# The last attention step and the first feed-forward blocks in an order of their own, and feed-forward products in groups of four

## The reference

```python
def attn(x):      # linear attention, 32 heads of 8
    q, k, v = split(relu(x @ qkv_weight.T))
    vk = einsum('bnhe,bnhd->bhed', concat(v, 1), k)
    o = einsum('bhed,bnhd->bnhe', vk, q)
    return (o[..., :8] / (o[..., 8:] + 1e-15)) @ proj_weight.T + proj_bias

def xattn(x, ctx):    # softmax attention over the context, 16 heads of 16, rotary positions
    q, k, v = rope(x @ Wq.T), rope(ctx @ Wk.T), ctx @ Wv.T
    return softmax(q @ k.T * 0.25) @ v @ Wo.T + bo

def ffn(x):       # both layers of low rank: 256 -> 64 -> 1024 -> 64 -> 256
    P = x @ U1
    H = gelu(P @ V1 + b1)          # tanh form
    return (H @ U2) @ V2 + b2

x = layernorm(x + attn(x))
x = layernorm(x + xattn(x, ctx))
x = layernorm(x + ffn(x))
```

## Time and profile before

| | |
|---|---|
| time, median of 3 runs | 579.31 us (578.76 to 579.71) |
| profiled execution, its time | 579.79 us |
| its span in the trace | 578.0 us |
| TensorE busy | 517.7 us, 90% |
| VectorE, GpSimd, ScalarE busy | 390.9, 341.1, 319.4 us |
| mean granted TensorE clock | 0.963 |

### The profile page before, as it was taken

How to read it: one execution, slowest core, us unless ns; L and a number is a source line. 1 busy time by engine, 2 the same in 40 slices (tenths; PEclk the granted TensorE clock), 3 DMA queues, 4 the chain that set the end, 5 groups by cost and what they waited for, 6 DMA issues and landing times.

```text
span 578.0 us, 11456 instructions
## 1 busy us (share of the span) xinstructions
PE 517.7 (90%) x4044; PEld 350.5 (61%) x4044; DVE 390.9 (68%) x870; ACT 319.4 (55%) x457; POOL 341.1 (59%) x391
## 2 busy tenths in 40 slices
PE   6995998999999999999999999999777786899992
PEld 3884666666767676767667676767453343555551
DVE  6468786878787878778787878787776331334444
ACT  3452556565666656575656566565564562455641
POOL 6567266595959595766858595948553312242424
PEclk9999899999999999999999999999797798899998
DMA  8653111203021211112030202111010010122322
GB/s 270 140 109 82 43 34 57 69 7 100 10 78 32 77 51 36 59 49 88 5 102 10 78 30 78 33 38 33 1 33 20 2 54 18 55 99 100 110 92 108
DMA packets 29128, 35.96 MB, mean 62 GB/s; under 512 B 5720, under 2 KB 15320, under 8 KB 29080
## 3 DMA queue, kind: packets, MB, share of 16 engines
q1 hardware_dynamic: 28216, 34.37, 19.8%
q10 hardware_dynamic: 864, 0.95, 0.7%
HBM read 23.51 MB, written 8.65 MB: 56 GB/s over the span
## 4 chain that ended last, share of the span: by engine, by line
PE 60%; DVE 15%; issue 13%; POOL 5%; ACT 5%; DMA 1%; POOLq 1%; SPq 0%; DVEq 0%; ACTq 0%
PE FR L1187 21%; PE BK L1353 10%; PE BK L1187 8%; DVE nmax L1006 5%; PE SC L1310 5%; PE SC L1338 4%; PE FR L1270 3%; PE FR L1262 3%; PE FR L1381 3%; DVE lin_tm L916 2%; POOL rs L630 2%; POOL c_fm L635 2%; PE SC L1187 2%; DVE x_fm_l L993 2%; DVE rden L912 1%
## 5 line engine op out<-in xcount | busy, mean ns | idle before, releaser
L738 ACT ACTIVATE probs<-SC 128x1024 f32<-128x1024 f32 x128 | 131.1, 1024 | 103.1 <-PE SC L1338 103.0
L1006 DVE TENSOR_REDUCE nmax<-SC 128x4 f32<-128x1024 f32 x128 | 155.9, 1219 | 24.9 <-PE SC L1310 23.8
L1353 PE MATMUL BK<-probs,v_aug 128*32 128x256 f32 x1024 | 71.1, 396 | 0.6 <-ACT probs L738 0.6
L543 POOL TENSOR_TENSOR rs<-ve,minus_half 128x2 f32<-128x2 f32 x16 | 11.2, 701 | 94.3 <-DVE nm L1054 94.3
L1310 PE MATMUL SC<-k_blk,q_grp 48*128 48x512 f16 x256 | 51.2, 397 | 15.6 <-DVE nmax L1006 15.6
L1338 PE MATMUL SC<-q_grp,k_blk 64*128 64x256 f16 x512 | 51.1, 278 | 4.3 <-ACT probs L738 2.2
L827 ACT ACTIVATE probs<-SC,b_ff 128x512 f32<-128x512 f32 x64 | 39.9, 685 | 24.1 <-PE SC L1535 23.2
L1353 PEld LDWEIGHTS BK<-probs,v_aug 128*32 128x32 f32 x1024 | 27.1, 111 | 26.8 <-issue 15.5
L630 POOL TENSOR_TENSOR rs<-ve,minus_half 128x2 f32<-128x2 f32 x16 | 11.0, 689 | 47.8 <-DVE nm L1175 47.8
L1338 PEld LDWEIGHTS SC<-q_grp,k_blk 64*128 64x128 f16 x512 | 25.1, 97 | 22.7 <-ACT probs L738 6.2
L1545 PE MATMUL FR<-probs,w_u 128*64 128x512 f32 x128 | 36.7, 628 | 0.7 <-ACT probs L827 0.7
(11 more groups left out here) (229 smaller groups left out, 1546.1 us busy)
## 6 DMA issues: line engine op xcount, KB each, us to landing
x_fm<-in_x_fm SPq DMA_DIRECT2D x16, 256.0 KB, 5.4
x_tm<-in_x_tm SPq DMA_DIRECT2D x16, 256.0 KB, 5.1
x_kept<-x2b SPq DMA_DIRECT2D x16, 256.0 KB, 2.3
x_tm<-x_kept SPq DMA_DIRECT2D x16, 256.0 KB, 2.7
out<-c_fm SPq DMA_DIRECT2D x16, 256.0 KB, 2.0
c_fm<-in_c_fm SPq DMA_DIRECT2D x15, 256.0 KB, 5.8
k_blk<-k_rope SPq DMA_DIRECT2D x128, 16.0 KB, 1.8
cos_t<-rope_tables SPq DMA_DIRECT2D x8, 128.0 KB
```

The lines of the kernel that those rows point to most:

```text
L738: act.activation(probs[:, j % 4], SB[:], ACT.Exp, scale=SCALE).then_inc(s_exp, 1)
L1006: dve.tensor_reduce(nmax[:, t, :, 2 * q:2 * q + 2], src[:].rearrange("p (s f) t -> p s f t", s=2), AX.X, ALU.max, negate=True).then_inc(s_ ...
L1353: mm = pe.matmul(BK[q // 2][HP * k:HP * (k + 1), (q % 2) * T:(q % 2 + 1) * T], v_aug[b % NB][:, t, HC * q + k], probs[:, j % 4, k], start= ...
```

## The change

- The last step of the first stage (sequence 15) is taken out of the loop of steps and written out for each engine (`last_step`). In it the scores of chunk j go to `SC[j % 2]`, SA and SB in turn, and wait for exp j-2 instead of exp j-1. The parts of sequences 13 and 14 get other places; `wo(14)` writes FR[0] instead of BK[1].
- Feed-forward blocks 0 and 1 are both written out, mixed with the end of sequences 14 and 15; the loop starts at block 2. The two products of `h_ff(0, 0)` and `(0, 1)` stand before `pv(15, 6)` and `pv(15, 7)`. The gelu table is loaded by an instruction of its own behind the last exp.
- In a block, TensorE's order becomes h 0 to 3 of block i, u2 4 to 7 of block i-1, h 4 to 7 of i, v2 of i-1, u2 0 to 3 of i. Each u2 product has its own `wait_apart`. `ev_qf(i-1)` moves behind gelu 3 of block i.
- `gel` takes all of `probs`: eight buffers.
- VectorE's `ev_p(15)` moves behind block 0; the counts of s_y3, s_qf_ev and s_u2_mm start at zero.

The diff (without the 8 spaces that all its lines begin with):

```diff
@@ -182,7 +182,7 @@
-gel = probs[:].rearrange("p s h t -> p s (h t)")[:, :, 0:FB]
+gel = early.rearrange("p (g t) -> p g t", t=FB)
 qf_fm = [t[:].rearrange("p c t -> p (c t)") for t in xs_fm]
 x2_blk = x_tm
 y3 = x_fm
@@ -427,7 +427,7 @@
     def ffn_block(i, more=True):
         for h in range(2):
             if more:
-                sp.wait_ge(s_y3, 2 * i + h + 3)
+                sp.wait_ge(s_y3, 2 * i + h + 1)
                 fetch(i + 1, h)
         for h in range(2):
             sp.wait_ge(s_y, 4 * i + 2 * h + 2)
@@ -614,12 +614,16 @@
     weights_lo(V1, s_ff_lo)
     weights_lo(DD2, s_ff_lo)
     residual_bias(2)
-    for b in range(B):
+    for b in range(LAST):
         step(b)
+    norm2(LAST - 2)
+    att_scale(LAST - 1)
+    att_lo(LAST - 1)
+    keep_x2(LAST - 2)
     att_scale(LAST)
     norm2(LAST - 1)
+    att_lo(LAST)
     keep_x2(LAST - 1)
-    att_lo(LAST)
     norm2(LAST)
     keep_x2(LAST)
@@ -735,7 +739,7 @@
             act.wait_ge(s_ff_lo, 2)
         act.wait_ge(s_s2_mm, NQ * b + j + 1)
         wait(act, s_pv_mm, NQ * b + j - 3)
-        act.activation(probs[:, j % 4], SB[:], ACT.Exp, scale=SCALE).then_inc(s_exp, 1)
+        act.activation(probs[:, j % 4], (SC[j % 2] if b == LAST else SB)[:], ACT.Exp, scale=SCALE).then_inc(s_exp, 1)
     def step(b):
         n, m, p, q = b + 2, b + 3, b - 1, b - 2
@@ -817,38 +821,62 @@
     ev_x1(1, FR[1])
     ev_q2(1)
     ev_lint(2, FR[1])
-    for b in range(B):
+    def last_step():
+        exp_chunk(LAST - 1, 7)
+        ev_shift(LAST)
+        exp_chunk(LAST, 0)
+        exp_chunk(LAST, 1)
+        ev_x2t(LAST - 2)
+        exp_chunk(LAST, 2)
+        exp_chunk(LAST, 3)
+        ev_p(LAST - 2)
+        exp_chunk(LAST, 4)
+        ev_att(LAST - 1)
+        exp_chunk(LAST, 5)
+        exp_chunk(LAST, 6)
+        exp_chunk(LAST, 7)
+    for b in range(LAST):
         step(b)
-    exp_chunk(LAST, 7)
+    last_step()
+    act.preload_act_table(ACT.Gelu_apprx_tanh)
     act.sem_inc(s_gelu, 4)
     def gelu(i, f):
-        wait(act, s_u2_mm, NF * i + f + 1)
+        if not isinstance(i, int) or i > 0:
+            act.wait_ge(s_u2_mm, NF * i - NF + f + 1)
         act.wait_ge(s_h_mm, NF * i + f + 1)
-        act.activation(gel[:, f % 4], SC[f % 4 // 2][:].rearrange("p h t -> p (h t)")[
+        act.activation(gel[:, f], SC[f % 4 // 2][:].rearrange("p h t -> p (h t)")[
             :, FB * (f % 2):FB * (f % 2) + FB], ACT.Gelu_apprx_tanh,
             bias=b_ff1[:, f:f + 1]).then_inc(s_gelu, 1)
     def ev_qf(i):
-        act.wait_ge(s_u2_mm, NF * i + NF + 4)
+        act.wait_ge(s_u2_mm, NF * i + NF)
         act.activation(qf_fm[0][:], FR[0][:], ACT.Copy).then_inc(s_qf_hi, 1)
+    act.wait_ge(s_pv_mm, NQ * B - 2)
+    for f in range(4):
+        gelu(0, f)
     act.wait_ge(s_pv_mm, NQ * B)
-    gelu(0, 0)
-    gelu(0, 1)
+    gelu(0, 4)
     ev_att(LAST)
-    for f in range(2, 6):
+    for f in range(5, NF):
         gelu(0, f)
     ev_x2t(LAST - 1)
-    gelu(0, 6)
     ev_p(LAST - 1)
-    gelu(0, 7)
+    for f in range(4):
+        gelu(1, f)
+    ev_qf(0)
+    for f in range(4, NF):
+        gelu(1, f)
     ev_x2t(LAST)
     ev_p(LAST)
-    with act.Fori(1, NFB) as i:
+    with act.Fori(2, NFB) as i:
+        for f in range(4):
+            gelu(i, f)
         ev_qf(i - 1)
-        for f in range(NF):
+        for f in range(4, NF):
             gelu(i, f)
     ev_qf(NFB - 1)
@@ -1041,11 +1069,11 @@
         wait(dve, s_attt_ev, p)
         dve.transpose(flat(att_raw[:]), flat(lin_tm[:])).then_inc(s_att_raw, 1)
-    def add2(p):
+    def add2(p, src=BK[1]):
         dve.wait_ge(s_wo_mm, p + 1)
         dve.wait_ge(s_x1b, p + 1)
         wait(dve, s_x2, 2 * p)
-        dve.tensor_tensor(y2[:], BK[1][:].rearrange("p (t c) -> p t c", t=TT), x1b[:, p % NB], ALU.add
+        dve.tensor_tensor(y2[:], src[:].rearrange("p (t c) -> p t c", t=TT), x1b[:, p % NB], ALU.add
                           ).then_inc(s_wo_ev, 1)
     def stats2(p):
@@ -1145,18 +1173,23 @@
     row_max(0, 6)
     row_max(0, 7, SB)
     shift(0)
-    for b in range(B):
+    for b in range(LAST):
         step(b)
-    dve.sem_inc(s_qf_ev, 1)
-    dve.sem_inc(s_y3, 2)
+    ev_shift(LAST)
+    stats2(LAST - 2)
+    turn_pv(LAST - 1, 1)
+    att_norm(LAST - 1)
+    att_turn(LAST - 1)
+    ev_p(LAST - 2)
+    turn_pv(LAST, 0)
+    add2(LAST - 1, FR[0])
     turn_pv(LAST, 1)
     att_norm(LAST)
+    stats2(LAST - 1)
     att_turn(LAST)
-    stats2(LAST - 1)
+    ev_p(LAST - 1)
     add2(LAST)
-    ev_p(LAST - 1)
     stats2(LAST)
-    ev_p(LAST)
     def ffn_block(i):
         dve.wait_ge(s_qf_hi, i + 1)
@@ -1170,10 +1203,11 @@
             dve.tensor_tensor(y3[:, h], BK[h][:].rearrange("p (t c) -> p t c", t=TT), x2_blk[:, h], ALU.add
                               ).then_inc(s_y3, 1)
         for h in range(2):
-            stats(y3[:, h], (s_y3, 2 * i + h + 3), st3[:, h], s_st3, mv3[:, h], s_mv3, 4 * i + 2 * h)
+            stats(y3[:, h], (s_y3, 2 * i + h + 1), st3[:, h], s_st3, mv3[:, h], s_mv3, 4 * i + 2 * h)
             dve.tensor_scalar(ve3[:, h], mv3[:, h, :, 1], LN_EPS, None, ALU.add).then_inc(s_ve3, 1)
             dve.tensor_scalar(nm3[:, h], mv3[:, h, :, 0], -1.0, None, ALU.mult).then_inc(s_ve3, 1)
     ffn_block(0)
+    ev_p(LAST)
     with dve.Fori(1, NFB) as i:
         ffn_block(i)
@@ -1329,13 +1363,17 @@
     def scores2(b, j):
         q, t = j // 2, j % 2
+        out = SC[j % 2] if b == LAST else SB
         if j == 0:
             pe.wait_ge(s_shift_ev, 2 * b + 2)
-        wait(pe, s_exp, NQ * b + j)
+        if b < LAST:
+            wait(pe, s_exp, NQ * b + j)
+        elif j > 0:
+            pe.wait_ge(s_exp, NQ * b + j - 1)
         for f in range(2):
             for s in range(2):
                 rows = slice(TR * s, TR * (s + 1))
-                mm = pe.matmul(SB[:, 2 * s + f], k_blk[b % NB][rows, q, f, t * P:(t + 1) * P],
+                mm = pe.matmul(out[:, 2 * s + f], k_blk[b % NB][rows, q, f, t * P:(t + 1) * P],
                                q_grp[b % NB][rows, q], start=True, stop=True)
         mm.then_inc(s_s2_mm, 1)
@@ -1347,20 +1385,24 @@
             pe.wait_ge(s_v2_ev, min(b + 2, B))
             if on(b + 3):
                 pe.wait_ge(s_q1_ev, b + 4)
-        if j == 4:
+            if b == LAST:
+                pe.wait_ge(s_pvc_ev, b)
+        if j == 4 and b < LAST:
             wait(pe, s_wo_ev, b)
+        elif j == 4:
+            pe.wait_ge(s_pvd_ev, b)
         for k in range(HC):
             mm = pe.matmul(BK[q // 2][HP * k:HP * (k + 1), (q % 2) * T:(q % 2 + 1) * T],
                            v_aug[b % NB][:, t, HC * q + k], probs[:, j % 4, k],
                            start=(t == 0), stop=(t == TT - 1))
         mm.then_inc(s_pv_mm, 1)
-    def wo(p):
+    def wo(p, out=BK[1]):
         if p == 0:
             pe.wait_ge(s_qo_lo, 2)
         pe.wait_ge(s_attt_ev, p + 1)
         for t in range(TT):
-            mm = project(BK[1], att_fm, w_o2, t)
+            mm = project(out, att_fm, w_o2, t)
         mm.then_inc(s_wo_mm, 1)
     def x2_t(q):
@@ -1518,13 +1560,33 @@
     scores1(0, 6)
     scores1(0, 7)
     proj1(2)
-    for b in range(B):
+    def last_step():
+        scores2(LAST - 1, 7)
+        shift_t(LAST)
+        scores2(LAST, 0)
+        scores2(LAST, 1)
+        pv(LAST - 1, 6)
+        pv(LAST - 1, 7)
+        scores2(LAST, 2)
+        x2_t(LAST - 2)
+        scores2(LAST, 3)
+        pv(LAST, 0)
+        pv(LAST, 1)
+        p_ff(LAST - 2)
+        scores2(LAST, 4)
+        scores2(LAST, 5)
+        pv(LAST, 2)
+        pv(LAST, 3)
+        scores2(LAST, 6)
+        scores2(LAST, 7)
+        pv(LAST, 4)
+        pv(LAST, 5)
+        wo(LAST - 1, FR[0])
+    for b in range(LAST):
         step(b)
-    scores2(LAST, 7)
-    pv(LAST, 6)
-    pv(LAST, 7)
-    pe.sem_inc(s_u2_mm, 4)
+    last_step()
     pe.wait_ge(s_ff_lo, 2)
     def h_ff(i, f):
@@ -1536,20 +1598,29 @@
                            start=(k == 0), stop=(k == 1))
         mm.then_inc(s_h_mm, 1)
-    def u2_ff(i, f):
-        for k in range(2):
-            pe.wait_ge(s_gelu, NF * i + f + k + 5)
-            if f + k == 0:
-                pe.wait_ge(s_qf_ev, i + 1)
-            pe.matmul(FR[0][R * k:R * k + R, :], w_u2[:, f + k], gel[:, (f + k) % 4],
-                      start=(f == 0), stop=(f == NF - 2)).then_inc(s_u2_mm, 1)
+    def h_ff4(i, half):
+        for f in range(4 * half, 4 * half + 4):
+            h_ff(i, f)
+    def u2_ff4(i, half):
+        if half == 0 and isinstance(i, int) and i == 0:
+            pe.wait_ge(s_wo_ev, LAST)
+        elif half == 0:
+            pe.wait_ge(s_qf_ev, i)
+        for f in range(4 * half, 4 * half + 4):
+            wait_apart(pe, s_gelu, NF * i + f + 5)
+            pe.matmul(FR[0][R * (f % 2):R * (f % 2) + R, :], w_u2[:, f], gel[:, f],
+                      start=(f < 2), stop=(f >= NF - 2)).then_inc(s_u2_mm, 1)
     def v2_ff(i):
-        pe.wait_ge(s_qf_ev, i + 2)
+        pe.wait_ge(s_qf_ev, i + 1)
```

(44 more changed lines are left out.)

## The result

The median is **556.34 us** (four executions, 555.81 to 557.4) against 579.43 before (four): ratio 0.9605, 95% interval 0.9587 to 0.9623. The forecast was 564.8, in a range from 561.3 to 569.0. The direction was right, and the change gave 23.1 us where 14.5 were forecast. The profiled execution took 557.4 us, the slowest of its four, 1.06 above the median.

The account below looks back on a forecast made before the run. Order bound the stretch from 452 to 501, TensorE's own work the loop. The last block's u2 end moved from 566.0 to 550.0, 16.0 us raw; less 0.7 and 0.8, gain 14.5: forecast 564.8 us, range 561.3 to 569.0.

Parts of the forecast that it names:

- the signs of being wrong: ScalarE idle over 2 us between exps 3 and 4, u2 group over 2.5 us, or v2, `wo(15)`, `x2_t(15)` waiting.
- The last step: Sequence 15's eight exps: alternating score buffers and written order end them at 466.0 against 470.72, 4.7 us earlier.
- Last exp to the first qf copy: Stretch behind the last step: table load right behind the last exp, one TensorE wait; 17.3 us against 26.22 before.
- the hole of 1.7: TensorE's single wait, before the transpose of sequence 14, for POOL's norm ready at 474.1: 1.7 us.
- the 1.5 us given back: Taken off the raw gain of 16.0 us: 0.7 for uncounted handovers, 0.8 for half clock behind TensorE's wait.
- The loop: Feed-forward blocks on TensorE: 9.64 us against 9.88, fewer changes between h and u2, each u2 group about 2.03.
- The bound: Cross-check from 452.3 to 566.0: TensorE's work at full clock is 91.3 us, so no order gains over 22.4.
- A: Whole kernel, the forecast itself: the new order holds, 562.5 to 567 us; chance 60%.
- B: Behind the last exp: load 1.46 us late, TensorE at half clock twice more, 568.8 us; chance 20%.
- C: Feed-forward blocks get no shorter, or slip because qf's low half comes late: 566.5 us; chance 8%.
- D: Last step: exps stay 2.3 us apart as ScalarE waits for `x2_t` and `p_ff`; 4.7 us lost, 569.5; chance 7%.
- E: u2 products: the semaphore instruction stops pairs overlapping, 0.6 x 32 pairs = 19 us, 584 us; chance 5%.

Follow-up runs that it names:

- filler: Changed kernel with five unused products of 512 columns on TensorE behind `shift_t(15)`, in the lull before the last step: 556.83 us median.
- v2 later: Kernel before, with v2 of the block before placed behind h 6-7 instead of h 4-5 in the loop: 580.81 us median, ratio 1.0043.
- the statistics early: Changed kernel with `stats2(14)`, `norm2(14)` and `ev_x2t(14)` moved ahead of `turn_pv(15, 1)`, `att_scale(15)` and gelus 5 to 7: 554.45 us median.
- the best kernel: Changed kernel with statistics of 14 ahead of the turn of 15, no table load of its own, `ev_x2t(13)` behind exp 2: 554.23 us median, ratio 0.9595.
- the one-buffer run: Changed kernel with the last step's scores all in SB, waiting for exp j-1 again, written order kept: 560.37 us median, ratio 0.9679.

## Why the prediction was wrong

**The reading of what bounds** was right. The order ahead of the loop carried the most (7.0 + 9.0 of 22.4 us), and the loop is bound by TensorE. The range reached down to 561.3 by allowing for no handovers, no clock fall and a last step 2 us shorter, and all three came true. What took the time below it is the loop, for which the range had nothing, and 2.0 us of clock and of the profiled executions' places (1.4 and 0.6). None of the signs of being wrong showed: ScalarE idled 0.45 us between exps 3 and 4, a u2 group took 1.87, and neither v2 nor `wo(15)` nor `x2_t(15)` waited. All of them looked for a slower kernel, none for a faster one.

**The last step**: mechanism right, the term mis-sized. I took half clock up to 460.6 "as before". In the profile it was 3.4 us, in seven others of the two-buffer order without filler none. ScalarE's stops shrank with TensorE's products: `p_ff` was at its result 1.1 us after its start where I had 2.08, the pair of pv products took 1.3 where I had 1.9. Step 11.05 us, 10.15 at full clock, forecast 13.3. That the order itself prevents the fall is not shown: the filler could not tell, and when the clock falls differs between executions of one kernel. For it speaks that in the last step all three profiles of the old order have 10.2 us at half clock, while of the ten of the new order two have 3.4 and eight none. That 3.4 us at half clock cost 0.9 us here is shown by two executions of the same kernel.

**Last exp to the first qf copy**: 17.3 forecast, 17.20 measured, with the hole of 1.7 at 1.65. That the sum agrees this well is in part luck: the transpose of 14 came 8.4 us behind the last exp, not 8.1, and the work from there was 0.4 us shorter than priced. The load behind the last exp began at once. The drain of some 1380 ns that the Trainium skill gives for a table switch ("ScalarE: Activation LUTs", What ACT_TABLE_LOAD costs) did not show: 0.01 us lie between exp and load. The clock did not fall behind the hole, nor there in any of the ten profiles of the new order, so 0.8 of the 1.5 us given back was wrong, and the 0.7 for handovers did not come either. That the product of `wo(15)` comes late enough to hide its chain held.

**The loop**: this is the step that failed, the largest share of the miss. "u2 2.03" was read from the earlier trace rows as the work of four products. It was work and a wait: gelu 7 ended 0.16 us too late, and in a pipelined group such a wait shows as busy time. The true price is 1.87, measured in the old order (v2 later) and in the new. Two groups a block make 0.32 of the 0.35 us between 9.64 and 9.29. Over six blocks that is 2.1 us. Of the remaining 0.6, two groups outside the loop, taken at 2.0 us, make 0.26; the transpose of 15 (0.53 us where 0.65 was taken) and rounding make the rest. The prices worked out from these runs (1.87 and 1.01 for two pairs and one, 2.72 with one pair in the same half, 66.24 less 64.11 over six blocks): two overlapping products 0.855 us, a group's own cost 0.16, a change between h and u2 products with its group 0.355.

**The bound** "no order could gain more than 22.4" was too low, but this change doesn't show it. It was put on the stretch from the first exp of sequence 15 to the last `ev_qf`; there the change gained 21.0 us (113.4 to 92.4), and the other 1.4 of the span lie ahead of it. With the statistics early the stretch was 89.6, in the best kernel 89.2: gains of 23.8 and 24.2. The bound had eight blocks at 9.45 us; at 9.29 they are 1.3 less, which is most of what it missed.

**Ahead of the change**: nothing was forecast, and 1.4 us came. Up to 406 the two profiles are within 0.13 us of each other; they part by the clock's fall between 408 and 416, 3.4 us long in one and 6.8 in the other, and both lengths occur among profiles of the new order.

**The rivals.** A: the order held, but the time came out below its 562.5. B (lulls stay): no fall between the last exp and the last `ev_qf`, though the hole of 1.65 us was there, and the load came at once. C: the loop got 0.59 us a block shorter, not less than 0.24; its slip is what v2 later showed when VectorE is made late. D: ScalarE's stops for `x2_t(13)` and `p_ff(13)` were 1.29 and 0.45 us, and the 4.7 us were not lost; the one-buffer run loses a similar 4.2, but by another wait, that for the scores. E: no overlap was lost; had it been, 32 pairs at 0.85 would have cost 27 us, not 19.

## What to carry to other kernels

A group of products in a busy stretch is not its work: compare its duration with one more and one less product, and look when each input was ready, before using it as a price. Moving work out of a hole costs what the hole hid: count what covers the wait afterwards. Compare stretches between common events, not totals, when the clock of one engine differs from execution to execution by more than the effect.

## What the runs showed of the hardware

- The same kernel ran from 571.8 to 579.5 us of span with its mean granted TensorE clock from 0.978 to 0.960. Ahead of the last `ev_qf`, stretches at 1.2 GHz were 3.4, 6.8 or 10.2 us long, 17 to 44 us in all per profile.
- Two float32 products of 512 columns into opposite 64-column halves take 0.855 us together, and 1.71 into the same half, worked out from groups of four (1.87 us, and 2.72 with one pair in the same half) and of two (1.01).
- The gelu table load takes 1.28 us. Given behind the last exp, it starts within 0.02 us of its end; given in front of a gelu whose input is ready (the kernel before, no load of its own), the gelu follows within 0.02 us of the load.
- A semaphore instruction between products in opposite halves costs nothing and leaves their overlap: the block takes 9.29 us with and without it.
